# A new written-out order of steps, banks and engines for a fused attention and expert kernel

## What is computed

```python
# first block, on layernorm(x)
q = (h @ Wq.T).astype(bf16);  k = (h @ Wk.T).astype(bf16)
q = rope(q, pos, 32.0);       k = rope(k, pos, 32.0)
scores = q @ k.T / 128 ** 0.5
exp_qk = where(causal, exp(scores), 0.0)
o = relu(exp_qk.sum(-1) @ fc1_w.T + fc1_b) @ fc2_w.T + fc2_b
x = x + layernorm(o)
# second block, on layernorm(x): only expert 1 has weight
y = relu(h @ W1[1] + b1[1]) @ W2[1] + b2[1]
x = x + layernorm(y)
```

## Time and profile before

| | us |
|---|---|
| median of 3 timed runs (lowest, highest) | 93.51 (92.78, 93.65) |
| the profiled execution, its own time | 92.26 |
| its span, first to last instruction | 90.5 |
| PE busy | 82.5 |
| DVE busy | 77.8 |
| ACT busy | 73.0 |
| GpSimd busy | 55.8 |

### The profile page before, as it was taken

One profiled execution on the slowest core, in us unless ns is written; L12 is line 12 of the kernel. 1 busy time (PEld: TensorE's weight loads), 2 busy tenths in 40 slices (PEclk: granted clock), 3 DMA queues, 4 the chain that ended last, 5 costly groups with the idle time before them and its releaser, 6 DMA issues.

```text
span 90.5 us, 1552 instructions
## 1 busy us (share of the span) xinstructions
PE 82.5 (91%) x452; PEld 51.0 (56%) x458; DVE 77.8 (86%) x220; ACT 73.0 (81%) x205; POOL 55.8 (62%) x71
## 2 busy tenths in 40 slices
...
GB/s 41 264 234 277 262 202 69 245 214 122 86 34 33 83 0 120 0 0 0 7 0 116 116 0 0 0 116 4 7 0 0 0 24 211 0 0 116 100 132 116
DMA packets 11714, 7.58 MB, mean 84 GB/s; under 512 B 806, under 2 KB 10810, under 8 KB 11706
## 3 DMA queue, kind: packets, MB, share of 16 engines
...
...
## 4 chain that ended last, share of the span: by engine, by line
PE 60%; ACT 16%; DVE 12%; issue 3%; DMA 3%; POOL 2%; POOLq 1%; SPq 1%; DVEq 0%
PE psum L738 17%; PE psum L788 14%; ACT psum L544 10%; PE psum L752 9%; PE psum L712 6%; PE psum L774 5%; PE psum L685 4%; DMA rot<-qk 3%; DVE rot L371 3%; ACT qk L461 2%; POOL rstd L451 2%; PE psum L782 2%; DVE x_s L663 2%; DVE b_s L672 2%; DVE rot L387 2%
## 5 line engine op out<-in xcount | busy, mean ns | idle before, releaser
L451 POOL TENSOR_TENSOR rstd<-mv,half_neg 128x4 f32<-128x4 f32 (+1 forms) x36 | 34.5, 963 | 29.2 <-DVE mv L530 24.1
L544 ACT ACTIVATE psum<-psum 128x1024 f32<-128x1024 f32 (+7 forms) x48 | 36.9, 768 | 1.0 <-PE psum L757 0.5
L752 PE MATMUL psum<-rot 128*128 128x512 bf16 (+3 forms) x74 | 19.4, 346 | 0.9 <-ACT qk L461 0.4
L738 PE MATMUL psum<-cols_n,wqk 128*128 128x512 f32 (+1 forms) x36 | 16.6, 555 | 0.1
L738 PE MATMUL psum<-cols_n,w_c 128*128 128x512 f32 (+1 forms) x36 | 16.3, 554 | 0.0
L788 PEld LDWEIGHTS psum<-w_c,hid 128*128 128x128 f32 x128 | 15.6, 192 | 1.1 <-issue 0.7
L788 PE MATMUL psum<-w_c,hid 128*128 128x128 f32 x128 | 15.7, 275 | 0.0
L752 PEld LDWEIGHTS psum<-rot 128*128 128x128 bf16 x80 | 7.0, 98 | 11.8 <-ACT psum L544 6.0
L520 DVE BATCH_NORM_STATS2 stats<-psum 128x6 f32<-128x256 f32 x24 | 9.2, 419 | 1.4 <-PE psum L788 1.4
L663 DVE SCALAR_TENSOR_TENSOR x_s<-psum,rstd,x 128x128 f32<-128x128 f32 x32 | 9.1, 343 | 1.4 <-POOL rstd L451 1.4
L712 PE MATMUL psum<-ident,rows_n 128*128 128x128 f32 x60 | 9.3, 275 | 0.7 <-DVE qk L461 0.6
...
## 6 DMA issues: line engine op xcount, KB each, us to landing
...
```

Of the source, the lines that this page charges most:

```text
L451: ready[k].done(eng.tensor_tensor(rstd[:, g, slot[k], t], mv[:, g, slot[k], t, 1], half_neg[:, 0:tiles], ALU.pow), n)
L544: exps.done(eng.activation(bank[:, 0:width], bank[:, 0:width], ACT.Exp, scale=scale_qk, accum_out=sums[:, g, s, j:j + 1]), n, j, s)
L738: made[name].done(eng.matmul(banks.of(name, n)[:, 0:tiles * P], weight, cols_n[:, g, c], start=True, stop=True), n)
L752: mm = eng.matmul(bank[:, at:at + width], query, qk_r[:, g0 + c, 1, 0:width], start=True, stop=c < gb)
```

## The change

`STEPS` is replaced by another order of the same 483 words; no other line of the kernel changes. The new list has another order on every engine, other banks for many matmuls, and another engine letter at 43 steps. The first two rows and two later ones of the list:

```diff
-mask.0 repeat.0 load_x.0 load_x.5 load_wqk.0 load_x.1 swapneg.0 load_x.2 stat1.0 blank.4 tr1.0@6 load_fc.0 var1.0
-+tr1.0.A rstd1.0 load_table.0.0 stat1.5 blank.3 wqk.0@5 load_w2.0 var1.5 tr1.1@6 stat1.1 load_x.4 spread.0@4 rstd1.5
+mask.0 repeat.0 load_x.0 load_x.2 load_wqk.0 load_x.1 swapneg.0 load_x.5 stat1.0 blank.4 tr1.0@6 load_table.0.0 var1.0
++tr1.0.A rstd1.0 load_fc.0 stat1.2 blank.3 wqk.0@0 load_x.4 var1.2 tr1.1@2 stat1.1 load_x.7 spread.0@5 rstd1.2
...
-tr1.7@7 exp.1.3.0 cos.3.D fc2.0@0 +tr1.7.D cos.4.P scores.4.2.1@6 exp.1.2.0 scores.4.3.1@5 part3.0.D scores.4.0.1@4
+tr1.7@7 b2split.0 +q.3.D +hT.0 exp.1.0.0 scores.1.3.0@3 +tr1.7.D swap.3 fc2.0@5 exp.1.3.0 sin.5.D scores.1.2.0@0 q.4@7
...
```

More of the change, by code:

```diff
@@ L51 @@
[L51 to L55, removed]
@@ L61 @@
[L61 to L65, removed]
@@ L66 @@
-exp.5.2.1 stat4.1 exp.5.3.1 var4.1 exp.5.1.1 hT.2@1 scores.6.2.1@4 rstd4.1 part5.0.D +hT.2 scores.6.1.0@6 exp.6.2.1
-tr1.8@3 stat5.0.D rstd5.0 fc2.2@0 +tr1.8.D exp.6.1.0 scores.6.3.0@4 part3.2.D norm4.1.P k.8@3 exp.6.3.0 stat3.2.D
-out.0 fc2.4@6 rstd3.2 +k.8.A scores.5.0.1@5 trz.1@4 part3.4.D store.0 exp.5.0.1 scores.5.1.0@2 +trz.1.A q.8@5
-stat3.4.D x1.2 rstd3.4 exp.5.1.0 h1.1@4 +q.8.A stat4.2 scores.5.3.0@2 +h1.1.A swap.8 x1.4 h0.1@1 exp.5.3.0
-scores.6.0.0@4 var4.2 +h0.1.D rstd4.2 scores.5.0.0@6 exp.6.0.0 scores.3.0.0@2 cos.8.D y.1@1 stat4.4 norm4.2.P
```

55 lines of the change are left out of this document (35 added, 20 removed).

## The result

The changed kernel took 93.84 us (median of 20 runs, 93.27 to 95.08) against 92.89 (20 runs, 92.51 to 94.17): a ratio of 1.0091 with a 95% interval of 1.0059 to 1.0123. Forecast was 91.8. By the ratio, which leaves out each kernel's slow runs, it is 0.85 us slower, by the two medians 0.95, where 1.7 faster was expected. Its profiled execution took 93.74 us.

What follows compares the result with a forecast made beforehand. PE was taken to bound the kernel, with only its idle time ahead of 40.4 us to win. Terms -1.4 - 0.3 + 0 + 0 = -1.7 us from a 93.51 median give 91.8 us; range 90.0 to 93.9.

Steps and rivals of the forecast that it cites:

- Term 1: 12.8 to 24.1 us: blocked VectorE excess goes, PE leads at the first fc2; -1.4 us, bounds -2.5 and 0.
- the walk of 2.5: 12.8 to 24.1 us: walking all queues with nothing lost at hand-overs gives PE a lead of 2.5 us.
- lower bound's worry: 12.8 to 24.1 us: no lead (0) where ACT or a landing transfer takes VectorE's place.
- Term 2: 24.1 to 40.4 us: y.0's wait for b2rows goes, cos.6 can catch the third cast; -0.3 us, between -0.9 and +1.3.
- Term 3: 40.4 to 86.1 us: PE has 0.2 us idle and no work goes; 0 taken, 0.6 gain to 1.0 loss.
- Term 4: Opening and tail: PE's first scores within 0.2 us, tail stays 4.4 us; 0 taken, between -0.3 and +0.4.
- Rival B: 24.1 to 40.4 us: lead given back as new bank waits, ACT and PE being full; no change, 93.0 us, chance 0.20.
- C: Three long GpSimd products (rope.3, cos.6, cos.8) block VectorE from the other side; slower, +1.7 us, 95.2, chance 0.12.
- C's three places: Third cast at b2rows waits 1.25 us, sin.5 at norm1.8 1.04, sum.1 behind rope.3 up to 1.1.
- rival A: Whole lead kept and growing, hand-overs also tight between 24 and 40 us; about 3.5 us earlier, 90.0 us, chance 0.20.

Runs made afterwards that it cites:

- e3: Kernel before with the first half table's load put ahead of fc's load; 92.92 us, ratio to before 0.999.
- e15: Kernel before with one letter changed, cos.4 on VectorE instead of GpSimd; 92.19 us, ratio to before 0.9884.
- e1: Changed kernel with the three one-row casts (b2rows.0) moved ahead of +w1.0, at about 24 us; 94.18 us, ratio to before 1.012.
- e5: Changed kernel with the three casts (b2rows.0) moved ahead of part3.1, at about 34 us; 93.78 us, ratio to before 1.0044.
- e9: Changed kernel with load_table.2 issued earlier, ahead of swap.2; 93.41 us, ratio to before 1.0049.
- e7: Changed kernel's order up to y.1 with e5's edit, then the order of the kernel before; 94.11 us, ratio to before 1.0107.
- e6: Changed kernel's order up to y.1, then the order of the kernel before, banks chosen anew; 95.69 us, ratio to before 1.0224.
- e17: Changed kernel with two letters of its back half changed, +h1.4 and norm4.5 to VectorE; 93.61 us, ratio to before 1.006.
- e14: Changed kernel with cos.6 on VectorE instead of GpSimd, casts left in place; 93.38 us, ratio to before 1.002.
- e16: Kernel before with e15's edit and the three casts (b2rows.0) moved ahead of rope.6; 91.45 us, ratio to before 0.9802.

## Why the prediction was wrong

Against e3 as the fair partner (same instructions in the same order on PE, VectorE, ACT and GpSimd as before), by the table:

- **Term 1, predicted -1.4, measured -1.9.** From x.1 to the first fc2 are 14.86 us (e3 18.35), 3.49 earlier, less the 1.57 us of matmuls put behind it: 1.92. "fc2.0 could then start at 20.5" came out as 20.85. The count of VectorE's steps held, between the value taken and the walk of 2.5. The blocked excess was the right thing to count, and e15 confirms it alone: 1.93 us of excess removed, 1.17 of PE time won. The prediction took each us of excess for one of PE's, which is more than e15 gives, so that the sum came this near is in part luck. Its lower bound's worry did appear, a landing table ahead of cos.5 (0.46 us here, 0.86 in e1, 0.98 in e5); without it the first fc2 comes 0.3 us earlier (e9), and by y.1 0.15.
- **Term 2, predicted -0.3, measured +0.7 up to y.0, where its stage ended, and +1.2 up to y.1.** From the first fc2 to y.0 are 19.19 us against 16.94, to y.1 31.11 against 28.31; of each 1.57 is the work put behind. The failed step reads "casts one and two are through when cos.6 starts and the third can be caught", from which I drew "near the gain". The trace has exactly this: casts of 0.21, 0.22 and 1.19 us. I had described the event that came and then priced it by the two casts that got through, when the price is set by the one that did not. Yet it is not all of the term: with the casts elsewhere 0.32 us comes back by y.1 (e5), 0.44 in the second profile of that order (e7). The other 0.8 us were not pinned. PE's wait of 0.53 us for an exponential at 33.82, and VectorE's of 0.40 us for x1.1's power, which e1 and e5 both show once the casts are out of the way, stand in that stretch, and neither was tested alone.
- **Term 3, predicted 0, measured +1.0 from y.1 on**, at its bound, and +1.5 from y.0, beyond it (y.0 to y.1 took 11.92 us against 11.37; by the rates of the earlier trace rows about 0.15 of this is matmul work that moved behind y.0, an estimate). The failed step is "PE had 0.2 us idle. No part of the work went, so at best 0.2 and some short hidden gaps", which takes the same matmuls to last equally long in any order, together with taking the middle between -0.6 and +1.0. They do not: the fc2 of two units side by side take 1.06 us and apart 1.26, and with the 0.1 us ahead of each group and behind it such neighbours make up about 0.7 of the 1.03 us; 0.18 is the wait of trz.5. And from a state without slack there was little room for gain and much for loss. Idle times and busy shares do not show it even now; the distance between equal marks does, and then the starts of single rows.
- **Term 4, predicted 0**: the tail behind the last y grew by 0.2 us (5.68 against 5.47), within its bounds; x.1 stood 0.27 later than in e3, which the executions and the openings share in a way that was not pinned.

Counted up to y.1 and from it on, the sum is -1.9 + 1.2 + 1.0 + 0.2 + 0.3 = +0.8 us; the two profiles differ by 0.93 and the medians by 0.95.

Rival B foretold that "the lead is given back as new bank waits", C that long GpSimd products would catch VectorE from the other side. Of C's three places only b2rows came fully, norm1.8 lengthened sin.5 from 0.68 to 0.87 (to 1.08 in e6 and e17), rope.3 caught nothing; C's mechanism is shown (e14), but with 0.3 us it does not decide. What B says of a give-back in the middle holds; that ACT's and PE's load force it does not, since in e15 and e16 the whole lead arrives. Of rival A, that the lead arrives and grows, the first half holds in these two, for another order: 1.17 us at the first fc2 and 1.19 at the last y in e15. I had also put the sum on a median of three runs (93.51) that was 0.6 us above that of twenty; that shifts the forecast to 91.2 and makes its error larger.
